# First attention: the sum of the back probabilities in the pooling's bank, transposes in pairs, two expert tiles in other banks; rstd between weight pieces, a rounding on ScalarE

## What is computed

```python
x = x + tanh(g_xattn[0]) * two_way_attention(layernorm(x), ctx)   # "first attention"
x = x + tanh(g_ffn[0])   * experts(layernorm(x))                  # router, top 2 of 8
x = x + tanh(g_xattn[1]) * attention_relu(layernorm(x), ctx)
x = x + tanh(g_ffn[1])   * mlp(layernorm(x))                      # ternary 256-1024-1024-1024-256
# two_way_attention, for each batch (1024 rows of x against 77 of the context):
char2sub = softmax(Qc @ Ks.T * s, -1) @ Vs           # rows of x look at the context
sub2char = softmax(Qs @ Kc.T * s, -1) @ Vc           # "back": 77 rows look at the 1024
sub2char = interpolate(sub2char, 1024)
gate = sigmoid([char2sub, sub2char] @ Wg.T + bg)
out  = gate * char2sub + (1 - gate) * sub2char
```

## Time and profile before

| | us |
|---|---|
| median of 3 runs | 1020.14 |
| lowest and highest | 1019.06, 1020.44 |
| the profiled execution | 1017.13 |
| its span, first to last instruction | 1015.3 |
| TensorE busy in the span | 987.0 (97%) |
| VectorE, ScalarE, GpSimd busy | 511.7, 465.5, 309.9 |
| mean granted clock of TensorE, share of 2.4 GHz | 0.997 |

### The profile page before, as it was taken

The page is one execution under the profiler, slowest core; times in us unless marked ns, Lnnn a source line. Parts: engine busy times, 40 slices in busy tenths (PEclk is TensorE's granted clock), DMA queues, the critical chain, the costliest instruction groups (busy, mean ns, idle before and its releaser), DMA issues.

```text
span 1015.3 us, 14179 instructions
## 1 busy us (share of the span) xinstructions
PE 987.0 (97%) x5138; PEld 818.6 (81%) x5138; DVE 511.7 (50%) x1394; ACT 465.5 (46%) x854; POOL 309.9 (31%) x444
## 2 busy tenths in 40 slices
PE   7998989899999999999999999999999999999997
PEld 4877777678789888887899887887888788788886
DVE  5678778886432554863332553451355355234311
ACT  1354445546444444444544445355344535534432
POOL 0125553411630514566110542311154322112111
PEclk9999999999999999999999999999999999999999
DMA  9930015703385444566656465363446545445551
GB/s 325 382 116 1 2 51 163 246 4 120 116 281 183 149 142 145 151 212 195 196 205 219 143 194 161 104 187 104 140 141 192 157 118 168 121 127 158 144 144 54
DMA packets 43979, 156.35 MB, mean 154 GB/s; under 512 B 6427, under 2 KB 7323, under 8 KB 43010
## 3 DMA queue, kind: packets, MB, share of 16 engines
q0 software_dynamic: 29952, 104.88, 34.1%
q1 hardware_dynamic: 10842, 39.19, 11.5%
q10 hardware_dynamic: 3112, 11.33, 2.8%
HBM read 136.49 MB, written 27.26 MB: 161 GB/s over the span
## 4 chain that ended last, share of the span: by engine, by line
PE 85%; DVE 6%; ACT 3%; issue 2%; POOL 2%; DMA 2%; SPq 0%; DVEq 0%; POOLq 0%; ACTq 0%
PE psum L1153 59%; PE psum L1047 2%; PE psum L825 2%; PE psum L939 2%; PE psum L1233 1%; PE psum L1235 1%; PE psum L1234 1%; PE psum L793 1%; PE psum L1073 1%; PE psum L1055 1%; PE psum L1208 1%; PE psum L949 1%; DVE x_normalised L1729 1%; PE psum L850 1%; DMA x_residual<-in_x 1%
## 5 line engine op out<-in xcount | busy, mean ns | idle before, releaser
L2489 POOL DMA_DIRECT2D mlp_pieces<-in_mlp x176 | 96.4, 554 | 434.7 <-PE psum L1153 432.1
L1153 PE MATMUL psum<-hidden_a_high,mlp_pieces 128*128 128x512 f32 x512 | 203.6, 398 | 0.2 <-DMA mlp_pieces<-in_mlp 0.2
L1153 PE MATMUL psum<-hidden_b_high,mlp_pieces 128*128 128x512 f32 x512 | 202.6, 396 | 0.0
L1153 PE MATMUL psum<-hidden_a_low,mlp_pieces 128*128 128x512 f32 x512 | 199.7, 390 | 0.0
L1153 PE MATMUL psum<-hidden_b_low,mlp_pieces 128*128 128x512 f32 x512 | 199.5, 390 | 0.0
L2311 DVE TENSOR_TENSOR hidden_a_low<-hidden_a,hidden_a_high 128x512 fp32r<-128x512 f32 x128 | 88.0, 687 | 165.3 <-ACT hidden_a_high L1639 164.4
L2311 DVE TENSOR_TENSOR hidden_b_low<-hidden_b,hidden_b_high 128x512 fp32r<-128x512 f32 x64 | 44.3, 693 | 170.7 <-ACT hidden_b_high L1639 170.7
L1153 PEld LDWEIGHTS psum<-hidden_a_high,mlp_pieces 128*128 128x128 f32 x512 | 96.2, 188 | 22.9 <-DVE hidden_a_low L2311 1.8
L1656 ACT ACTIVATE hidden_a<-psum,mlp_scales 128x512 f32<-128x512 f32 x64 | 44.1, 689 | 153.7 <-PE psum L1153 153.6
L1153 PEld LDWEIGHTS psum<-hidden_b_high,mlp_pieces 128*128 128x128 f32 x512 | 96.2, 188 | 20.2 <-issue 0.8
L1153 PEld LDWEIGHTS psum<-hidden_b_low,mlp_pieces 128*128 128x128 f32 x512 | 96.2, 188 | 20.1 <-issue 0.7
(11 more groups left out here) (296 smaller groups left out, 1791.2 us busy)
## 6 DMA issues: line engine op xcount, KB each, us to landing
mlp_pieces<-in_mlp POOLq DMA_DIRECT2D x176, 512.0 KB, 3.9
mlp_piece_to_examine<-in_mlp SPq DMA_DIRECT2D x17, 512.0 KB, 3.9
yrows<-expert_rows ACTq DMA_DIRECT2D x16, 512.0 KB, 3.0
slot_rows<-slots SPq DMA_DIRECT2D x14, 512.0 KB, 4.8
slots<-in_zeros SPq DMA_DIRECT2D x1, 5120.0 KB, 47.7
x_residual<-in_x SPq DMA_DIRECT2D x4, 1024.0 KB, 24.2
out<-x_residual SPq DMA_DIRECT2D x7, 512.0 KB, 3.5
slots<-in_zeros SPq DMA_DIRECT2D x1, 3072.0 KB, 33.7
```

Source lines behind the costliest of these rows:

```text
L1153: last = mm(o, a, b, start=(k == 0 and i == 0), stop=(k == n_k - 1 and i == len(parts) - 1))
L2489: pool.dma_start(mlp_ring[:, r % RING, :], d["mlp"][r % NCHECK]).then_inc(ring_in[r % RING], 16)
```

## The change

- `a_sum_back` writes the sum to column 6L of bank 6, behind the pooled columns, and waits for ScalarE's copy of these (`t2_v`); `a_sums` reads it there. `a_sub2char` on TensorE no longer waits for `rsr_r`; the scores of bank 6 in the next batch wait for `rsr_r` instead of `t2_v`.
- `a_turn` on TensorE and ScalarE goes by pairs of tiles: four transposes into one whole bank (4 or 5 by turns), one copy of 128x512.
- `turn_bank(0, j)` is 4 + j: tiles 2 and 3 of the first expert group go to banks 6 and 7. They wait for `rsr_r` and for `sf_v`. `a_probs_T(3)` waits for the low parts of tiles 0 and 1 alone.
- In `halve_context_weight` ScalarE makes both rounded copies: the first after the tanh of the last tile, the second before `c_turn(0)`. VectorE keeps the subtraction and makes it ahead of `c_norm(0)`.
- POOL issues three ring pieces, makes the inverse deviation of group 0, then issues the other two.

```diff
@@ -428,6 +428,7 @@
         xTc_r = sem("x_transposed_c_high_saved")
         xTl_r = sem("x_transposed_c_low_saved")
         w1_r = sem("context_weight_halves_ready")
+        w1c_r = sem("context_weight_rounded")
         xupc = sem("x_updated_c")
         stats_c = sem("ln_stats_c_ready")
         inv_c = sem("ln_rstd_c_ready")
@@ -528,7 +529,7 @@
 
         def turn_bank(g, j):
 
-            return 4 + j % 2 if g == 0 else j % 2
+            return 4 + j if g == 0 else j % 2
 
         def first_turn(g, j):
 
@@ -796,22 +797,26 @@
 
 
             def a_turn(c, tiles):
-                for j in tiles:
-                    pe.wait_ge(xn_r, c * JT + (j + 1))
-                    if j >= 2:
-                        pe.wait_ge(xT_r, c * JT + (j - 1))
+                for j in tiles[::2]:
+                    pe.wait_ge(xn_r, c * JT + (j + 2))
+                    if j >= 4:
+                        pe.wait_ge(xT_r, c * JT + (j - 2))
                     elif c == 0:
                         pe.wait_ge(map_v, 2)
                     else:
                         pe.wait_ge(e1_r, c * JT)
-                    transposes(xn[:, j, :], 4 + j % 2, tp)
+                    for k in range(KC):
+                        for i in range(2):
+                            last = pe.transpose(ps[:, 4 + j // 2 % 2, (2 * k + i) * P:(2 * k + i + 1) * P],
+                                                xn[:, j + i, k * P:(k + 1) * P], ident[:])
+                    last.then_inc(tp, 2)
 
             def a_both_scores(c, g):
                 pe.wait_ge(xT_r, (c + 1) * JT)
                 if c == 0:
                     pe.wait_ge(map_v, 6)
                 elif g == 2:
-                    pe.wait_ge(t2_v, c)
+                    pe.wait_ge(rsr_r, c)
                 else:
                     pe.wait_ge(p1t_v, 2 * c - 1 + g)
                     pe.wait_ge(p1l_v, 2 * c - 1 + g)
@@ -840,7 +845,8 @@
 
             def a_sum_back(c):
                 pe.wait_ge(sb2_r, c + 1)
-                mm(ps[0:L, 7, 2 * P:2 * P + 1], s1b[:], onec[:], start=True, stop=True).then_inc(rs_ps, 1)
+                pe.wait_ge(t2_v, c + 1)
+                mm(ps[0:L, 6, 6 * L:6 * L + 1], s1b[:], onec[:], start=True, stop=True).then_inc(rs_ps, 1)
 
             def a_pool(c, k):
                 for i, g in enumerate(BANKS):
@@ -855,7 +861,6 @@
                 if c == 0:
                     pe.wait_ge(fw_v, 2)
                 pe.wait_ge(t2_v, c + 1)
-                pe.wait_ge(rsr_r, c + 1)
                 for h, w in enumerate(("Wv_cT", "Wv_c")):
                     for k in range(KC):
                         last = mm(ps[0:L, 7, h * D:(h + 1) * D], t2T[:, k, :], wa(w)[:, k, :],
@@ -902,6 +907,10 @@
                     pe.wait_ge(xn_r, NT + 1 + j + G * g)
                     if first_turn(g, j):
                         pe.wait_ge(e1_r, NT)
+                    elif g == 0 and j == 2:
+                        pe.wait_ge(rsr_r, B)
+                    elif g == 0:
+                        pe.wait_ge(sf_v, 2 * B)
                     else:
                         pe.wait_ge(xT_r, NT - 1 + j + G * g)
                     transposes(xn[:, s * G + j, :], turn_bank(g, j), tp)
@@ -1024,7 +1033,7 @@
                     a_turn(c + 1, (6, 7))
                 a_sum(c - 1, 7)
                 if c == B - 1:
-                    pe.wait_ge(xT_r, NT + G)
+                    pe.wait_ge(xT_r, NT + 2)
                 a_probs_T(c)
             b_route_T(0, 0)
             pe.wait_ge(ua_r, NT - JT)
@@ -1387,11 +1396,11 @@
 
 
             def a_turn(c, tiles):
-                for j in tiles:
-                    act.wait_ge(tp, c * JT + (j + 1))
-                    act.activation(xnT[:, :, j * P:(j + 1) * P],
-                                   ps[:, 4 + j % 2, 0:D].rearrange("p (k c) -> p k c", k=KC), ACT.Copy
-                                   ).then_inc(xT_r, 1)
+                for j in tiles[::2]:
+                    act.wait_ge(tp, c * JT + (j + 2))
+                    act.activation(xnT[:, :, j * P:(j + 2) * P],
+                                   ps[:, 4 + j // 2 % 2, :].rearrange("p (k c) -> p k c", k=KC), ACT.Copy
+                                   ).then_inc(xT_r, 2)
 
             def a_exp_back(c):
                 for i, g in enumerate(BANKS):
@@ -1524,6 +1533,14 @@
                                    accum_out=lowsum[:, i:i + 1]).then_inc(ck_r, 1)
                     act.wait_ge(ck_r, i + 1)
 
+            def round_context_weight():
+                act.wait_ge(fin, NT)
+                act.activation(w1c[:], w1t[:], ACT.Copy).then_inc(w1c_r, 1)
+
+            def round_context_weight_in_place():
+                act.wait_ge(w1_r, 1)
+                act.activation(w1h[:], w1c[:].bitcast(F32), ACT.Copy).then_inc(w1_r, 1)
+
             def c_turn(c):
                 for pair in range(2):
                     act.wait_ge(tpc, 1 + pair + 2 * c)
@@ -1570,7 +1587,9 @@
             examine(range(10, 11))
             b_exp(1)
             a_sum(B - 1, 7)
+            round_context_weight()
             examine(range(11, 14))
+            round_context_weight_in_place()
             c_turn(0)
             examine(range(14, 16))
             c_project(0)
@@ -1848,7 +1867,7 @@
 
             def a_sums(c):
                 dve.wait_ge(rs_ps, c + 1)
-                st.link(dve.reciprocal(rs2[:, 3:4], ps[0:L, 7, 2 * P:2 * P + 1]))
+                st.link(dve.reciprocal(rs2[:, 3:4], ps[0:L, 6, 6 * L:6 * L + 1]))
                 dve.tensor_scalar(rgh[:], rs2[:, 3:4], gh[0:L, 0:1], None, ALU.mult).then_inc(rsr_r, 1)
 
             def a_inverse(c, q):
@@ -2078,11 +2097,8 @@
                                       xcT_h[:, :, t].bitcast(F32), ALU.subtract).then_inc(xTl_r, 1)
 
             def halve_context_weight():
-                st.link(dve.tensor_copy(w1c[:], w1t[:]))
+                dve.wait_ge(w1c_r, 1)
                 dve.tensor_tensor(w1l[:], w1t[:], w1c[:].bitcast(F32), ALU.subtract).then_inc(w1_r, 1)
-                dve.wait_ge(w1_r, 1)
-                dve.tensor_copy(w1h[:], w1c[:].bitcast(F32)).then_inc(w1_r, 1)
-                dve.wait_ge(w1_r, 2)
 
             def c_max(c):
                 dve.wait_ge(sb_ps, c + 1)
@@ -2140,8 +2156,9 @@
                 for m in range(G * E // 4 - 2):
                     b_add(g, s, m)
                     if m == 0:
+                        halve_context_weight()
                         c_norm(0)
-                        halve_context_weight()
+                        dve.wait_ge(w1_r, 2)
                         c_low(0)
                     if m == 1:
                         a_measure(B - 1, (6, 7))
@@ -2491,9 +2508,11 @@
             pool.wait_ge(fin, NT)
             pool.wait_ge(th_r, NT)
             pool.wait_ge(xupd, NT)
-            for r in range(RING):
+            for r in range(3):
                 load_piece(r)
             invert(0, G, STATS_A)
+            for r in range(3, RING):
+                load_piece(r)
             invert((B - 1) * JT + G, G, STATS_A + 1)
             invert(0, G, 1, stats_c, inv_c)
             invert(G, G, STATS_A + 2)
```

## The result

| | before | after |
|---|---|---|
| median of 4 runs each, side by side, us | 1019.86 | 1010.53 |
| lowest and highest | 1019.06, 1020.44 | 1009.04, 1011.73 |
| ratio, with its 95% interval | | 0.9918 (0.9906 to 0.9931) |
| the profiled execution, its span | 1017.13, 1015.3 | 1011.73, 1009.9 |
| its mean granted clock | 0.997 | 0.997 |

The changed kernel is 9.3 us faster in the medians, 5.4 us in this pair of profiled executions. Why these two differ is the main thing that was learned, and it is in large part a matter of TensorE's clock.

A forecast was written before the change was run, and what follows sets the result against it. The first 222 us, where engines work in turns, were taken to decide the gain. Terms 1.0 + 2.8 + 3.4 + 0.95 = 8.15 us, taken as 8.0, from the median 1020.14 gave 1012.1 us, range 1009.5 to 1016.3.

The forecast's parts named there:

- rival D: Whole kernel: the 3.0 us between profile and median are clock falls behind removed waits; gain 10, 1010 us; chance 0.08.
- Rival C: Batches 1 to 3: waits grow back, VectorE and ScalarE's order hold them; gain about 4, 1016 us; chance 0.14.
- What bounds the kernel: First 222 us, engines in turns: the gain is what these lose; TensorE's later 793 us block only moves whole.
- Sum in bank 6 and pairs: Batches 1 and 2: L861 without the inverse's wait and fewer hand-overs, 1.4 us each, 2.8 together, bounds 2.2 to 3.3.
- the same pattern: Batch 2 was taken to have batch 1's pattern of waits, so 1.4 us is gained there again.
- Start and batch 0: Pairs gain 0.4 us before the values product and 0.5 in batch 0, L861 0.1; sum 1.0, bounds 0.5 to 1.3.
- Batch 3: Two tiles in banks 6 and 7, earlier transposes and full clock until L928: 3.4 us, bounds 1.2 to 3.6.
- VectorE's shift: Batch 3: x_T_low moves with VectorE from 145.54 to 144.25, so the chain loses 1.3 us.
- the clock and the two banks: Batch 3: transposes no longer behind x_T_low 1.0 us, full clock 0.6 and 0.7, with 0.2 given back.
- Last pass: Rstd between pieces and rounding on ScalarE: L1047 starts at 196.95 instead of 197.89, 0.95 us, bounds 0.4 to 1.1.
- Rival B: Batch 3: the clock falls nevertheless, price 1.3 to 1.7 us, so 1013.7 us; chance 0.17.
- the last line of its sum: Whole kernel: 1009.1 us against the profile; the same difference applied to the median 1020.14 gives 1012.1 us.

The follow-up runs named there:

- two single kernels: The kernel before with only rstd after three of five pieces, or only the copies on ScalarE with the subtraction ahead: stage 16.58 and 16.74 us, before 17.42.
- idle products: The kernel before with 8, 5 and 5 unread products in TensorE's waits for the inverse in batches 1 to 3: 1016.33 against 1018.48 us, ratio 0.9983.
- two further kernels: Changed kernel with ScalarE's second-half normalising ahead of sub2char's high part; then also expert tiles 2 and 3 turned one product later: 1008.89 and 1008.17 us.
- second execution: A second profiled execution of the changed kernel, nothing altered: 1009.55 us, span 1007.7, clock 0.999.

## Why the prediction was right, and where it was not

1012.1 us was forecast, 1010.53 measured: inside the range, nearer to rival D (1010) than to the forecast. By stages 7.6 us went, of 8.15 that the terms gave and 8.0 that were taken; the median lost more than the stages. Rival C (waits grow back, 1016) came true in part: TensorE waits 2.1 us for x_normalised in front of L810, four times, where it waited 0.8 us in front of L734, and the stages below are what was left after that.

**What bounds the kernel** held: the block behind 222 us kept its length (817.4 us from `c_project` to the end in both), and all of the gain lies ahead of it.

**Sum in bank 6 and pairs.** Batch 1 came out as worked (-1.40). Counted from `a_probs_T(0)`, VectorE's L1882 starts at 21.75 us where 21.71 was worked out, and `a_probs_T(1)` at 26.19 for 26.11. Batch 2 gave 0.97 instead of 1.4, and the term that failed is that of the pairs, carried over as "the same pattern". The sum alone gave its 1.14 us in batch 2 as in batch 1, though L861 had waited only 1.28 us there against 2.05: the stage of the sum alone was 25.64 us. With the pairs it is 25.81, so they took back 0.17 where they had given 0.24 in batch 1 (26.38 to 26.14). The changed kernel's rows of batch 2:

```profile
114.07 0.60 ACT L1401 ACTIVATE x_normalised_T<-psum 128x512 f32<-128x512 f32 x1 [0.46 <-PE psum L810]
...
116.19 0.99 PE L876 MATMUL psum<-identity,probs 128*77 128x128 f32 x7 [0.41 <-ACT x_normalised_T L1401]
```

A pair's copy starts when both of its tiles are transposed. ScalarE idles 0.46 us for that at tiles 4 and 5 and is done with the last pair 0.41 us after TensorE could go on; with the sum alone it starts the single tile 4 at 113.74, and L871 follows the products of tile 7 without a wait. The prediction let ScalarE's chain of batch 2 run without this idle time. The further step that moves the normalising forward took this wait away (25.39 us).

**Start and batch 0**: 0.55 and 0.59 for 0.4 and 0.6. From the first transposes to the values product it is 0.70 less (2.84 for 3.54); the start of these transposes varies from 22.19 to 23.52 us among the traces.

**Batch 3**: 3.10 for 3.4. The mechanism was right, three sizes were off. VectorE's shift was 1.1 (the sum alone) for 1.3. The rest, 2.0 us for 2.1, is the clock and the two banks; the clock's share is about 1.4, by the same stages at either level (L871 to the router product 1.65 against 0.86 in the kernel with the pairs alone, the router products 2.10 against 1.47, the whole stage 32.15 against 30.77), where 1.3 was forecast. So the banks' own share is some 0.6, against 1.0 less 0.2: the wait on x_T_low didn't vanish, 0.74 us of it stand in front of L925.

**Last pass**: 0.99 for 0.95, and POOL's and VectorE's orders interlock as worked out; the text treated the two edits as one, and the two single kernels show why that was needed.

**The clock and the median.** Rival B, a fall in batch 3 nevertheless, did not come in any of the six traces that have both the sum and the two banks. But the prediction took a wrong step at the last line of its sum: it subtracted the gain from the median as if both kernels had the same falls elsewhere. The timed executions order by their mean clock:

| | mean clock, runs, mean us |
|---|---|
| before, 77 runs beside the experiments | 0.997: 12, 1016.9; 0.995 and 0.996: 50, 1018.8; 0.992 and 0.993: 15, 1020.9 |
| after, 10 runs | 0.999: 5, 1009.4; 0.997: 5, 1011.5 |

The traces put a number to these levels: no fall at 0.998 and 0.999, one at 0.997, two at 0.995 and 0.996, three at 0.993 (and two, one of them twice as long, at 0.994). So the profile of before, 1017.13 us with one fall, was the best sort of execution, the median has two, and the changed kernel has none or one. At one fall each the gain is 5.4 us (1016.9 to 1011.5); between the medians it is 8 to 9. The difference is about one and a half falls at 2 us (an estimate). That is rival D, given 0.08: the 3.0 us between profile and median were in large part falls behind waits that went with the change. It should have had more, since a profile 3 us ahead of its median was itself the sign, and the list of TensorE's waits named three candidates. The idle products show directly that falls hang on the three waits of L861. The kernels without pairs indicate that they don't go for good when a wait moves: they move with it. So the range held by the stages, which were nearly right, and the forecast of 1012.1 was 1.6 us off by what was left out of the clock; batch 2 and batch 3, 0.4 and 0.3 short, hid some of that.

The Trainium skill, "TensorE: Matmul & The Clock Gate" (Part 4: PE-mode transpose), has it that transposes don't count as busy for the gate in the same way. Batch 1 agrees in direction: of the three traces with a wait of 1.43 us and only transposes behind it two have a fall there, of the four with 0.84 none. It doesn't separate the transposes from the length of the wait, since no run put other products in their place. In the first expert pass seven ordinary products stand between the two waits, and in the two further kernels a wait of 1.3 us between transposes and router products brought no fall.

**Left open.** By stages a fall costs 1.35 to 1.5 us (31.14 against 29.67 in the first expert pass, 7.96 against 6.61 from L861 to L871), by the runs' levels 2.0; what makes up the rest no trace here shows. By stages the gain without the fall of batch 3 is 6.2 us (7.6 less 1.4), by the levels 5.4. And the sum alone had four of six runs at 0.997, though its trace has the same wait of 1.43 us in batch 1 as the kernels whose clock fell there. With six runs this can be chance. So its 5.4 us in the median don't show that it is better than the sum and the two tiles together (3.7 us); by stages the latter gain more.

## What to carry to other kernels

Compare the clock of the profiled execution with those of the timed runs before a gain is subtracted from a median: here the profile that was 3 us faster than its median had fewer falls, and a removed wait was worth its length and its falls. A wait that is moved has to be priced at its new place, clock included: the pairs, which shorten one of 1.43 us to 0.84, were worth 0.7 us at full clock (1010.1 against 1009.4), but 3.6 in the mean and 4.7 in the median. A copy for two tiles starts with the later tile: in batch 2 that cost more than the saved hand-over gave. Two edits that shorten parallel paths to the same product are priced together.

## What was not expected of the hardware

The same program with the same waits has its clock fall in some executions and not in others, 0 to 3 times in the 222 us of each trace, at different places: behind one wait of 1.28 us, 1.43, 1.53 or 2.06, and also behind two of 0.58 and 0.82 with 1.4 us of full work between them. A fall lasted 3.4 us, once 6.8. A wait of 2.05 us went without, and so did one of 1.3 us in all eleven runs of two kernels.

One addition on POOL took almost four times its usual length while VectorE worked without a gap:

```profile
83.83 0.73 POOL L2487 TENSOR_TENSOR x_residual<-x_residual,update_of_sub2char 128x256 f32<-128x256 f32 x1
...
86.57 2.73 POOL L2487 TENSOR_TENSOR x_residual<-x_residual,update_of_sub2char 128x256 f32<-128x256 f32 x1
```

The same addition takes 2.71 us in the second execution and 2.70 with the sum alone, but 0.73 in the kernel before, where VectorE idles from 86.11 to 87.23 and normalises only from 88.03 on. The 2.0 us more are as long as the stretch from 86.72 to 88.69 in which VectorE normalises four tiles and subtracts; no run tests whether one causes the other. It cost nothing here: no wait of TensorE in the list above is on POOL.
